# First and last mixture layers: experts rounded to 64 rows, 36 blocks with 4 shared ones; middle layer's shared-block weights copied on chip

## The chip, the cores and the metric

The kernel runs on one core of one Trainium2 chip. The metric is the device time of one execution in microseconds, lower is better. The chip's engines that matter here are TensorE (PE in the profile, its weight loads are PEld), VectorE (DVE), ScalarE (ACT), GpSimd (POOL) and SyncE (SP, which only issues transfers).

## The reference

Four layers over x of 4 x 512 tokens of 256 numbers; each adds an attention and then a feed-forward part. Three of the feed-forward parts are mixtures of experts in which every token goes to 2 experts:

```
x = x + attention(layernorm(x), ctx)                     # each layer has its own kind
# layers 0 and 3: 8 experts, hidden size F = 704 and 512
scores -> two experts per token, weights w0, w1
y = sum over the token's experts of w * (silu(t @ gate[e]) * (t @ up[e])) @ down[e]
x = x + y
# layer 1: 7 routed experts of F = 256 (the same form) and one shared expert that all tokens pass
# layer 2: one fp4-quantised feed-forward part, no experts
```

2048 tokens x 2 experts are 4096 (token, expert) pairs. All arithmetic of the experts is float32.

## The kernel before, in words

The stages run one behind another: `a0` (attention), `e0` (experts, F = 704), `a1`, `l1` (attentions), `e1` (experts, F = 256), `f2`, `a3`, `e3` (experts, F = 512). Between stages, and between the parts of a stage, all engines meet at a barrier.

**Routing** (`route`, tags e0r, e1r, e3r). VectorE works out for each pair a slot in a list of blocks of 128 rows, and for each block the expert that owns it (`owner`) and the token in each row (`token`). A matmul with one-hot matrices makes `token`. In e0 and e3 every expert's rows are rounded up to 128, which takes at most `ROUTED` = 39 blocks, each with one owner. The simple arithmetic for that stands at L2148 to L2163. In e1 a `Layout` of quarters (32 rows) is used: 34 blocks, of which 28 are whole and 6 are *mixed*: four experts with 32 rows each. Its arithmetic is longer (L2165 to L2197).

**Blocks of e0 and e3** (`blocks`, tags e0b, e3b). The down weights of all experts are kept in SBUF. Gate and up weights of one block's expert (F = 704: two transfers of 704 KB; F = 512: two of 512 KB) go into one of two buffers, `e0k_wgu` and `e0b_wgu` (e3k_wgu, e3b_wgu). SP waits until the up product of block n is done (`up_made`) and then reads the owner of block n+2 and issues its load (L1870 to L1872) into the buffer that block n has just left. PE does for block n: gate product (L2386, weights stationary and tokens moving, 128 columns at a time), transpose of the rows of block n+1 (L2380, `xp`), up product (L2386), down product of block n-1 (L2410, `yp`). ACT does silu of the gate (L2446), VectorE copies the turned rows (L2458), multiplies up by silu into `hT` (L2465), and weighs the result into `yb` (L2473). With F = 704 (`LEFT` is 64) the gate product of block n+1 waits for `h_done` of block n, since its bank also holds the last 64 columns of the up product. POOL fetches the rows of a block by an indirect transfer (L2345), its pairs' weights (L2351), and adds `yb` into `y_sum` by an indirect transfer that adds (L2359); each such send waits until the one before has landed. All four loops are hardware loops, the order of the blocks is 0, 1, 2, ... In e0, VectorE also does one `round` of fp4 quantisation for a later stage after every second block (18 in all).

**Blocks of e1** (`kept_blocks`, tag e1b). All experts' weights stay in SBUF (`e_kgu`, `kept_d`). Rows are stationary and weights move: a whole block takes two matmuls over 512 columns for gate and up (L2584), a mixed block eight, with 32 stationary columns each (L2581), and likewise for down (L2607, L2604). The four experts' weights of a mixed block are loaded again from HBM by SP into `e1b_mixed_gu`, `xn` and others (L2532), two sets at the beginning and then one behind each mixed block. POOL copies the row numbers to `e1b_index`, runs a filler instruction and fetches the rows (L2547 to L2550), from the first block on; ACT issues the stores of the results (L2639). PE runs 14 filler matmuls (`stay_busy`) first. The order of PE is gate and up of n, turn of the rows of n+1 (L2568), turn of the hidden rows of n-1 (L2594), down of n-2.

## Time and profile before

| | us |
|---|---|
| median of 3 runs | 1716.93 (1716.62 to 1720.66) |
| the profiled execution, whole | 1715.14 |
| its span, first to last instruction | 1713.2 |
| PE busy | 1485.6 (87%) |
| DVE, ACT, POOL busy | 945.3, 498.5, 485.1 |
| blocks of e0, first gate product to end of the last down product | 179.0 to 484.4 |
| blocks of e1, same | 974.1 to 1089.3 |
| blocks of e3, same | 1477.4 to 1695.2 |

The three stretches of blocks are 638 us of the span. The rest of the chip's time, 1.9 us of the profiled execution, lies outside the span. A timeline merges instructions of one line that follow one another: start, length, engine, line, what is written and read, how many, and in brackets the idle time of the engine before them with what ended it. One float32 product shows as two MATMUL records.

### The profile page before, as it was taken

What the parts mean: (1) busy time and instruction counts of PE and PEld (TensorE: products, weight loads), DVE (VectorE), ACT (ScalarE), POOL (GpSimd) and SP (SyncE); (2) the same over time, 40 slices, a digit from 0 to 9 for tenths busy, and PEclk for the clock granted to TensorE, in tenths of its full rate; (3) what the DMA queues carried; (4) which work ended last, traced back from release to release, by engine and by line L of the source; (5) the groups of instructions that cost most, each with busy time, mean ns of one, the idle gap of its engine ahead of it and who ended that gap; (6) DMA issues with size and microseconds to landing.
All of it is one profiled execution on the core that took longest, in us unless ns stands there. A gap on an engine that the chain in (4) does not pass through costs nothing. (4 is left out here: it accounts for less than half of the span.)

```text
span 1713.2 us, 33545 instructions
## 1 busy us (share of the span) xinstructions
PE 1485.6 (87%) x11942; PEld 1126.6 (66%) x11975; DVE 945.3 (55%) x2428; ACT 498.5 (29%) x1047; POOL 485.1 (28%) x585
## 2 busy tenths in 40 slices
PE   4887899999979986899978899677888797899995
PEld 3664799999968853455545455345666575699995
DVE  4556244444448968666637433489887556422221
ACT  2331111111147745465532122223331333011010
POOL 0102344444410002111112243342111110466663
PEclk9999999999988997899999999888899999999998
DMA  4209677777720005433305467210000004688885
GB/s 139 51 2 308 218 210 232 210 230 213 222 59 1 2 2 165 130 89 112 86 22 197 143 212 260 67 45 25 1 1 1 2 2 156 197 242 234 233 241 147
DMA packets 147445, 218.73 MB, mean 128 GB/s; under 512 B 21377, under 2 KB 96897, under 8 KB 147137
## 3 DMA queue, kind: packets, MB, share of 16 engines
q1 hardware_dynamic: 121792, 183.57, 32.9%
q0 software_dynamic: 20640, 29.16, 8.2%
q10 hardware_dynamic: 4896, 4.46, 0.8%
q8 instruction: 72, 1.18, 0.3%
q14 instruction: 45, 0.36, 0.1%
HBM read 184.59 MB, written 34.64 MB: 128 GB/s over the span
## 5 line engine op out<-in xcount | busy, mean ns | idle before, releaser
L1575 DVE TENSOR_REDUCE l1a_nm<-l1a_sc 128x1 f32<-128x512 f32 (+3 forms) x256 | 107.2, 483 | 53.6 <-PE l1a_sc L1711 53.6
L2446 ACT ACTIVATE e0b_sg<-e0b_gp 128x640 f32<-128x640 f32 x78 | 33.5, 481 | 266.1 <-PE e0b_gp L2386 266.1
L2359 POOL DMA_INDIRECT y_sum<-e0b_yb,e_token x39 | 63.1, 1619 | 140.5 <-DVE e0b_yb L2473 137.5
L2359 POOL DMA_INDIRECT y_sum<-e3b_yb,e_token x39 | 62.7, 1607 | 61.5 <-DVE e3b_yb L2473 58.6
L2446 ACT ACTIVATE e3b_sg<-e3b_gp 128x512 f32<-128x512 f32 x39 | 23.3, 597 | 189.5 <-PE e3b_gp L2386 189.5
L1709 PEld LDWEIGHTS l1a_sc<-l_stack_k,l_stack_q 128*128 128x128 bf16 x256 | 25.3, 99 | 60.9 <-issue 26.9
L1711 PE MATMUL l1a_sc<-causal_h,ident_h 128*128 128x128 bf16 x256 | 47.0, 223 | 19.9 <-PEq L1353 15.5
L2465 DVE TENSOR_TENSOR e0b_hT<-e0b_up,e0b_sg 128x640 f32<-128x640 f32 x39 | 32.2, 825 | 57.8 <-PE e0b_up L2386 57.8
L2753 POOL TENSOR_TENSOR f_hq<-f_q,f_q 128x704 f32<-128x704 f32 x16 | 22.9, 1432 | 135.7 <-DVE f_q L2740 135.7
L1470 POOL TENSOR_TENSOR xn<-xn 128x512 f32<-128x512 f32 x8 | 10.1, 1266 | 178.2 <-DVE xn L1438 178.2
L2386 PEld LDWEIGHTS e0b_gp<-e0b_xT,e0k_wgu 128*128 128x128 f32 x480 | 58.4, 197 | 1.9 <-DVE e0b_xT L2458 0.9
L1245 DVE TENSOR_REDUCE a_nm<-a_sc 128x8 f32<-128x512 f32 x64 | 39.7, 683 | 35.8 <-PE a_sc L1095 35.8
L2386 PE MATMUL e0b_gp<-e0b_xT,e0k_wgu 128*128 128x128 f32 x480 | 58.7, 281 | 0.5 <-DVE e0b_xT L2458 0.5
L2465 DVE TENSOR_TENSOR e3b_hT<-e3b_up,e3b_sg 128x512 f32<-128x512 f32 x39 | 27.0, 692 | 57.6 <-PE e3b_up L2386 57.6
L2584 PE MATMUL e1b_gu<-e_kgu,e1b_xT 128*128 x112 | 54.8, 613 | 1.8 <-DVE e1b_xT L2661 1.8
L1737 PE MATMUL l1a_st<-l_stack_q,l_stack_k 128*128 128x512 bf16 (+2 forms) x254 | 56.1, 302 | 0.0
L2386 PEld LDWEIGHTS e0b_gp<-e0b_xT,e0b_wgu 128*128 128x128 f32 x456 | 53.8, 192 | 2.5 <-issue 1.5
L2386 PE MATMUL e0b_gp<-e0b_xT,e0b_wgu 128*128 128x128 f32 x456 | 54.1, 276 | 1.4 <-DVE e0b_hT L2465 1.4
L2473 DVE TENSOR_SCALAR e0b_yb<-e0b_yp,e0k_weight 128x256 f32<-128x256 f32 x39 | 18.9, 484 | 62.4 <-PE e0b_yp L2410 62.4
L3236 PE MATMUL f_yp<-f2w_down,f_hT 128*128 128x256 f32 x192 | 49.1, 410 | 4.6 <-DVE x L3091 4.0
L1189 POOL CAST a_nmp<-a_nm 128x32 bf16<-128x32 f32 x16 | 8.9, 553 | 153.7 <-DVE a_nm L1245 153.7
L1709 PE MATMUL l1a_sc<-l_stack_k,l_stack_q 128*128 128x256 bf16 (+3 forms) x226 | 50.4, 297 | 1.8 <-DVE l1a_nm L1575 1.5
(637 smaller groups left out, 4015.1 us busy)
## 6 DMA issues: line engine op xcount, KB each, us to landing
e3k_wgu<-in_L_ffn_W SPq DMA_DIRECT2D x40, 512.0 KB
e3b_wgu<-in_L_ffn_W SPq DMA_DIRECT2D x38, 512.0 KB
e0k_wgu<-in_L_ffn_gate_proj SPq DMA_DIRECT2D x20, 704.0 KB
e0k_wgu<-in_L_ffn_up_proj SPq DMA_DIRECT2D x20, 704.0 KB
e0b_wgu<-in_L_ffn_gate_proj SPq DMA_DIRECT2D x19, 704.0 KB, 4.2
e0b_wgu<-in_L_ffn_up_proj SPq DMA_DIRECT2D x19, 704.0 KB, 5.5
x_rows<-xn SPq DMA_DIRECT2D x3, 2048.0 KB, 8.4
l_parts<-l1p_split SPq DMA_DIRECT2D x16, 384.0 KB, 3.1
```

What stands on the lines that cost most here:

```text
L1245: nc.vector.tensor_reduce(nm[:, :, r, :], bank[r][:].rearrange("p t (h l) -> p t h l", l=L), AX_X, ALU.max, negate=True).then_inc(max_done, 1)
L1575: nc.vector.tensor_reduce(nm[:, g % 2, q, i:i + 1], sc[q], AX_X, ALU.max, negate=True).then_inc(max_done, 1)
L1709: nc.tensor.matmul(sc[q], of_head(1, n)[:, q * P:(q + 1) * P], of_head(0, n)[:, 0:(q + 1) * P], start=True, stop=False)
L1711: last = nc.tensor.matmul(sc[q][:, q * P:(q + 1) * P], ident_h[:], causal_h[:], start=False, stop=True)
L1737: nc.tensor.matmul(to(k), of_head(0, n)[:, k * P:(k + 1) * P], of_head(1, n)[:, k * P:], start=False, stop=False)
L2359: pool.indirect_dma_start(y_sum, bass.IndirectOffsetOnAxis(ap=token[:, n:n + 1], axis=0), yb[n % 2][:], None, compute_op=ALU.add).then_inc ...
L2386: last = nc.tensor.matmul(dst[:, f, :], wgu[j][:, k, at + f * P:at + (f + 1) * P], xT[j][:, k, :], start=(k == 0), stop=(k == KC - 1))
L2446: last = nc.scalar.activation(sg[rows, chunks, :], gp[rows, chunks, :], ACT.Silu)
L2465: last = nc.vector.tensor_tensor(hT[j][rows, chunks, :], from_up, sg[rows, chunks, :], ALU.mult)
L2584: last = nc.tensor.matmul(gu[n % 2][:], xT[n % 2][:, k, :], wgu[:, bass.ds(e, 1), k, :].rearrange("p a f -> p (a f)"), start=(k == 0), sto ...
L2753: nc.gpsimd.tensor_tensor(v3(dst), v3(a[:, 0:n]), bcast(sc[:, 0:n // FP4_BLOCK], 2, FP4_BLOCK), ALU.mult).then_inc(result, 1)
L3236: last = nc.tensor.matmul(yp[:], hT[:, f, :], dT[:, f, :], start=(f == 0), stop=(f == FC - 1))
```

## The change

**Layout.** e0 and e3 get a `Layout` of halves: experts are rounded to 64 rows, 36 blocks, of which 32 are whole and 4 are mixed: rows 0 to 63 of one expert, rows 64 to 127 of another. The mixed blocks stand at places 4, 13, 22 and 31. Routing of e0 and e3 takes the longer arithmetic that e1 had, with 40 owners, and three more VectorE instructions for `plan.send`, the rows' targets per owner: in a mixed block each half is sent by an instruction of its own, the other half's rows going to a spare area.

**Blocks of e0 and e3.** All loops are written out. A *unit* is one owner's gate and up weights; there are 40 units for 36 blocks. Unit k goes to buffer k % 2 and its load waits for the up product of the block that used unit k-2. A mixed block n uses both buffers. Its gate and up products have the tokens stationary, 64 columns for each expert, and the weights moving, up to 512 columns; the hidden rows then have to be turned (`turn_hidden`, into a new bank `hp`), ACT copies them to `hT`, and the down product of block n follows at once, not one block later. Down weights of its two experts are copied in SBUF by ACT, piece by piece between the silus of the blocks before.

**Blocks of e1.** The layout stays (34 blocks, 6 mixed). The mixed blocks' weights are copied from the kept ones by ACT instead of being loaded; the stores are issued by SP; POOL's index copy and filler are gone; the rows of blocks 0 and 1 are fetched already in routing; the 14 filler matmuls are gone.

```diff
+HALVES = Layout(NE, P // 2)
+ROUTED = HALVES.blocks
...
+                        for n in range(2):
+                            pool.indirect_dma_start(first_rows[n][:], None, x_rows, bass.IndirectOffsetOnAxis(ap=token[:, n:n + 1], axis=0))\
...
-                    with sp.Fori(0, (NB - 3) // 2) as i:
-                        for j in (1, 0):
-                            step(i * 2 + 2 - j, j)
+                    for k in range(1, len(block_of)):
+                        if k >= 2:
+                            sp.wait_ge(up_made, block_of[k - 2] + 1)
+                        plan.load_gate_up(sp, owner, owner_of[k], k % 2)
...
+                        for i, (block_n, at, done, value) in enumerate(sent):
+                            if block_n == n:
+                                if i:
+                                    pool.wait_ge(*sent[i - 1][2:])
+                                pool.indirect_dma_start(y_sum, bass.IndirectOffsetOnAxis(ap=plan.send[:, at:at + 1], axis=0), yb[n % 2][:],
+                                                        None, compute_op=ALU.add).then_inc(done, 16)
...
+                                for k in range(KC):
+                                    for u, unit in enumerate(units_of[n]):
+                                        rows = slice(u * HALF, (u + 1) * HALF)
+                                        last = nc.tensor.matmul(flat(dst)[rows, lo:hi], xT[n % 2][:, k, rows],
+                                                                wgu[unit % 2][:, k, at + lo:at + hi], start=(k == 0), stop=(k == KC - 1))
...
+                        for unit in units_of[n]:
+                            pe.wait_ge(gu_in[unit % 2], 32 * (unit // 2 + 1))
...
+                        elif not is_mixed(n - 1):
+                            down(n - 1)
+                        if is_mixed(n):
+                            turn_hidden(n)
+                            down(n)
...
+                        for to, source in itertools.islice(pieces, 2 * FC // 3):
+                            nc.scalar.copy(to, source).then_inc(mixed_ready, 1)
...
-                        nc.gpsimd.tensor_copy(index[n % 2][:], token[:, order[n]:order[n] + 1]).then_inc(index_ready, 1)
-                        pool.wait_ge(index_ready, n + 1)
-                        nc.gpsimd.tensor_tensor(spare[:], const("place"), const("place"), ALU.add)
...
-                    stay_busy(gu[0][:], 14)
...
-                        if n >= 3:
-                            store(n - 3)
+                        if n in mixed_at and following:
+                            pieces = set_of(following[0])
+                        if following:
+                            copy_some(pieces, -(-OF_SET // (mixed_at[following[0]] - 1 - (mixed_at[following[0] - 1] if following[0] else 0))))
```

PE in e3, before: one block of the written-out first pass of the loop, which all blocks repeat. `gp` and `up` are the banks of the gate and up products, `inner` and `xnT` hold the kept down weights.

```order
L2386 MATMUL e3b_gp<-e3b_xT,e3b_wgu 128x128 x8
L2403 TENSOR_LOAD e_owner
L2403 ISA x2
L2380 MATMUL e3b_xp<-consts,e3k_xb 128x128 x2
L2386 MATMUL e3b_up<-e3b_xT,e3b_wgu 128x128 x8
L2410 ISA
L2410 MATMUL e3b_yp<-inner,e3b_hT 128x256
```

PE in e3 of the change, at the first mixed block: from the end of the down product of block 2 to the gate product of block 5.

```order
L2447 MATMUL e3b_yp<-xnT,e3b_hT 128x256
L2403 MATMUL e3b_gp<-e3k_wgu,e3b_xT 64x512
L2403 MATMUL e3b_gp<-e3b_wgu,e3b_xT 64x512
...
L2393 MATMUL e3b_xp<-consts,e3k_xb 128x128 x2
L2403 MATMUL e3b_up<-e3k_wgu,e3b_xT 64x512
...
L2447 MATMUL e3b_yp<-xnT,e3b_hT 128x256
L2429 MATMUL e3b_hp<-consts,first_weights 128x128 x4
L2441 MATMUL e3b_yp<-first_weights,e3b_hT 64x256 x8
L2408 MATMUL e3b_gp<-e3b_xT,e3k_wgu 128x128 x8
```

The mixed block reads both weight buffers from its first gate matmuls on, the turn and the down product of its own follow the down product of block 3, and nothing but the turn of block 6's rows stands between the gate and up products of block 5 and the gate product of block 6.

ACT in e1, before, at the first blocks: silu (L2646), copy of the turned hidden rows (L2635), store.

```order
L2646 ACTIVATE e1b_sg<-e1b_gu 128x256 x2
L2635 COPY e1b_hT<-e1b_hp 128x256
L2646 ACTIVATE e1b_sg<-e1b_gu 128x256
L2635 COPY e1b_hT<-e1b_hp 128x256
L2639 DMA y_slots<-e1b_yb 128x256
```

ACT in e1 of the change, the same place; behind the first silu come six copies of 512 columns, behind the second six of 256.

```order
L2685 TENSOR_LOAD e_owner
L2685 ISA x2
...
L2697 COPY e1b_mixed_gu<-e_kgu 128x512
L2707 ACTIVATE e1b_sg<-e1b_gu 128x256
L2697 ISA
L2697 COPY e1b_mixed_gu<-e_kgu 128x512
...
L2707 ACTIVATE e1b_sg<-e1b_gu 128x256
L2680 COPY e1b_hT<-e1b_hp 128x256
L2697 ISA
L2697 COPY e1b_mixed_d<-inner 128x256
```

The silus and copies of the hidden rows now stand behind up to six weight copies, and no store is left on ACT.

## Rows read from the trace of the kernel before

**Rows 1.** Timeline of PE, e0: start, length, what, idle before.

```profile
178.99 4.67 PE L2386 MATMUL e0b_gp<-e0b_xT,e0k_wgu 128*128 128x128 f32 x24 [0.52 <-DVE e0b_xT L2458]
...
187.50 2.92 PE L2386 MATMUL e0b_gp<-e0b_xT,e0b_wgu 128*128 128x128 f32 x24 [1.39 <-DVE e0b_hT L2465]
...
195.30 2.84 PE L2386 MATMUL e0b_gp<-e0b_xT,e0k_wgu 128*128 128x128 f32 x24
...
200.42 1.03 PE L2410 MATMUL e0b_yp<-inner,e0b_hT 128*128 x4
...
203.02 2.84 PE L2386 MATMUL e0b_gp<-e0b_xT,e0b_wgu 128*128 128x128 f32 x24
```

**Rows 2.** Timeline of PE, e3, down product to gate product one block on.

```profile
1491.93 1.03 PE L2410 MATMUL e3b_yp<-inner,e3b_hT 128*128 x4
...
1493.66 1.95 PE L2386 MATMUL e3b_gp<-e3b_xT,e3b_wgu 128*128 128x128 f32 x16
1495.45 0.38 PE L2380 MATMUL e3b_xp<-consts,e3k_xb 128*128 128x128 f32 x2
1495.67 1.95 PE L2386 MATMUL e3b_up<-e3b_xT,e3b_wgu 128*128 128x128 f32 x16
1497.45 1.03 PE L2410 MATMUL e3b_yp<-inner,e3b_hT 128*128 x4
```

**Rows 3.** Timeline of SP, e3: the next issue of weights.

```profile
1492.95 0.89 SPq L1872 DMA_DIRECT2D e3k_wgu<-in_L_ffn_W  x2
```

**Rows 4.** Chain that ended last, e3's beginning: start, length, what.

```profile
1476.36 0.38 SPq L1872
...
1476.85 4.83 DMA e3b_wgu<-in_L_ffn_W
```

**Rows 5.** Transfers by issuer: count, KB each, median us to landing.

```profile
e0b_wgu<-in_L_ffn_up_proj SPq DMA_DIRECT2D x19, 704.0 KB, 5.5
...
y_sum<-e3b_yb,e_token POOLq DMA_INDIRECT x39, 4.4
e1b_xb<-x_rows,e1b_index POOLq DMA_INDIRECT x34, 4.3
```

**Rows 6.** Timeline of PE, e1.

```profile
974.05 3.34 PE L2584 MATMUL e1b_gu<-e_kgu,e1b_xT 128*128 x4 [0.81 <-DVE e1b_xT L2661]
...
988.50 1.92 PE L2581 MATMUL e1b_gu<-e1b_mixed_gu,e1b_xT 128*32 128x512 f32 x16
...
991.72 1.88 PE L2584 MATMUL e1b_gu<-e_kgu,e1b_xT 128*128 x4
...
994.74 1.88 PE L2584 MATMUL e1b_gu<-e_kgu,e1b_xT 128*128 x4
...
1084.06 1.92 PE L2581 MATMUL e1b_gu<-xn,e1b_xT 128*32 128x512 f32 x16
```

**Rows 7.** Timeline of e1's beginning: fillers, first rows fetched and turned.

```profile
966.02 3.19 PE L359 MATMUL e1b_gu<-ones_h,ident_h 128*128 128x512 bf16 x14 [1.74 <-PEq L2003]
...
972.81 0.44 PE L2568 MATMUL e1b_xp<-consts,e1b_xb 128*128 128x128 f32 x2 [3.59 <-DMA e1b_xb<-x_rows,e1b_index]
```

**Rows 8.** Timeline of DVE: counts to owners, e0's routing, then e1's.

```profile
152.83 0.17 DVE L2148 COPY e0r_cnt<-e0r_small 128x8 f32<-128x8 f32 x1 [1.11 <-PE e0r_small L2020]
...
156.24 0.17 DVE L2221 CAST e_owner<-e0r_own 128x39 int32<-128x39 f32 x1
...
935.80 0.16 DVE L2165 TENSOR_SCALAR e1r_held_i<-e1r_small 128x8 uint32<-128x8 f32 x1
...
941.45 0.21 DVE L2225 TENSOR_TENSOR e_owner<-e1r_own,e1r_wrap 128x52 int32<-128x52 f32 x1
```

**Rows 9.** Groups of ACT: count, busy us, mean ns, idle before.

```profile
L2446 ACT ACTIVATE e0b_sg<-e0b_gp 128x640 f32<-128x640 f32 x39 | 27.4, 703 | 266.1 <-PE e0b_gp L2386 266.1
L2635 ACT COPY e1b_hT<-e1b_hp 128x256 f32<-128x256 f32 x34 | 12.7, 372 | 9.0 <-PE e1b_hp L2594 7.8
...
L1413 ACT CAST l1p_split<-xn 128x512 bf16<-128x512 f32 x16 | 9.4, 613 | 0.7 <-DVE xn L1447 0.5
```

More of the change, by code:

```diff
@@ L8 @@
+import itertools
 from contextlib import ExitStack
@@ L2397, in up_product @@
-                    def up_product(n, j):
-                        if positive(n):
+                        product(0, FC, gp, n, gate_made)
+                    def up_product(n):
+                        if n:
                             pe.wait_ge(h_done, n)
-                        product(F + LEFT, FULL, up, j, up_made)
-                    def expert(n):
-                        return pe.value_load(owner[0:1, bass.ds(n, 1)], min_val=0, max_val=plan.E - 1)
-                    def down(n, j, e):
-                        if positive(n):
-                            pe.wait_ge(y_copied, n)
-                        pe.wait_ge(h_done, n + 1)
-                        for f in range(FC):
-                            last = nc.tensor.matmul(yp[:], hT[j][:, f, :],
-                                                    plan.wd[f // 2][:, bass.ds(e, 1), f % 2, :].rearrange("p a d -> p (a d)"),
-                                                    start=(f == 0), stop=(f == FC - 1))
-                        last.then_inc(y_made, 1)
@@ L2415, in body @@
-                    def body(i, last_block=False):
-                        for j in (1, 0):
-                            n = i * 2 + 2 - j
-                            gate(n, j, i + 2 - j)
-                            e = expert(n - 1)
-                            if not (last_block and j == 0):
-                                turn_rows(n + 1, 1 - j, i + 2)
-                            up_product(n, j)
-                            down(n - 1, 1 - j, e)
-                    stay_busy(gp[:, 0:4, :].rearrange("p f c -> p (f c)"), 4)
@@ L2426, in _ @@
[L2426 to L2437 removed]
+                        product(F + LEFT, FULL, up, n, up_made)
@@ L2439, in _, with weights_of @@
+                    if not is_mixed(NB - 1):
+                        down(NB - 1)
                 @block.scalar
                 def _(act):
+                    def weights_of(i):
+                        for u, at in enumerate(lay.owner_at(order[mixed_at[i]])):
+                            e = act.value_load(owner[0:1, at:at + 1], min_val=0, max_val=plan.E - 1)
+                            for f in range(FC):
+                                yield mixed_d[u][:, f * D:(f + 1) * D], \
+                                    plan.wd[f // 2][:, bass.ds(e, 1), f % 2, :].rearrange("p a d -> p (a d)")
@@ L2445, in silu, with copy_hidden @@
+                        last.then_inc(sg_done, 1)
+                    def copy_hidden(n):
+                        act.wait_ge(h_turned, mixed_at.index(n) + 1)
                         for rows, chunks in PIECES:
-                            last = nc.scalar.activation(sg[rows, chunks, :], gp[rows, chunks, :], ACT.Silu)
-                        last.then_inc(sg_done, 1)
+                            last = nc.scalar.copy(hT[n % 2][rows, chunks, :], hp[rows, chunks, :])
+                        last.then_inc(h_done, 1)
@@ L2489, in _ @@
-                    body(0)
-                    with dve.Fori(1, NB // 2 - 1) as i:
-                        body(i)
-                    body(NB // 2 - 1, last_block=True)
-                    weigh_out(NB - 1, 0, NB // 2)
-    def kept_blocks(tag, wgu, wd, kept, F, lay, experts_n, owner, token, weights):
+                    copy_rows(0)
+                    for n in range(NB):
+                        if n + 1 < NB:
+                            copy_rows(n + 1)
+                        hidden(n)
+                        if n >= 1 and not is_mixed(n - 1):
+                            weigh_out(n - 1)
+                        if is_mixed(n):
+                            weigh_out(n)
+                        if rounds is not None and n % 2:
+                            rounds.round(dve, n // 2)
@@ L2510, in kept_blocks @@
             xp, hp = ps("xp", [P, 2 * KC, P]), ps("hp", [P, 2 * FC, P])
[L2511 to L2512 removed]
+            before = list(blocks_before)
+            blocks_before[0] += (NB + 1) // 2
+            blocks_before[1] += NB // 2
             mixed_gu = [tmp("mixed_gu", [P, PER, KC, 2 * F]),
```

465 lines of the change are left out of this document (251 added, 214 removed).

## The prediction

> **What bounds the kernel now.** I read three views, in this order: the timeline of PE through the blocks of e0 and e3, the issue of weights by SP beside it, and the same for e1. In e0 a block is 7.72 us of PE from one gate product to the next (195.30 to 203.02) with no idle time inside; its down product is the last 2.60 us of it (200.42 to 203.02) [rows 1]. In e3 a block is 5.52 us: down 1.73 (1491.93 to 1493.66), gate, turn and up 3.79 (to 1497.45), of these gate 1.79, turn 0.22, up 1.78, and then the next down [rows 2]. So there PE is the bound, block after block, and a block saved is worth its PE time, as long as everything that PE needs is there. What it needs from HBM is the block's weights. They are issued 1.02 us after the up product before (1491.93 to 1492.95) [rows 2, 3], and land 5.3 us after the first issue (1476.36 to 1476.85 + 4.83 = 1481.68) [rows 4]. In e0 the second of the two transfers takes 5.5 us from its own issue [rows 5], which comes some 0.5 us after the first, as SP needs 0.89 us for two [rows 3]: 6.0 us. Today this is hidden, because the load for block n+2 starts at the end of the up product of block n and has a down product and a whole block to run: 1.73 + 5.52 = 7.25 us in e3 against 1.02 + 5.3 and a wake-up of some 0.25, 6.6 us. The cover is only 0.7 us long. That margin is the centre of this prediction.
>
> e1 is not at its PE limit: a whole block is 3.02 us when nothing is missing (991.72 to 994.74), 3.22 when mixed (988.50 to 991.72), but from the first gate product to that of the last block, 33 blocks, it takes 110.0 us (974.05 to 1084.06) [rows 6], 3.33 each; rows land only 4.3 us after issue there [rows 5], and behind an index copy and a filler on POOL. It also begins late: PE's fillers start at 966.02, the first rows are there at 972.81 after 3.59 us of idle time [rows 7], and the first gate product runs at 974.05 and takes 3.34 us instead of 1.88 [rows 6].
>
> **Blocks saved.** 39 become 36: 3 x 7.72 = 23.2 us in e0 and 3 x 5.52 = 16.6 us in e3 come off [rows 1, 2]. A mixed block streams as many columns in total per half as a whole one if its two halves run side by side. No row shows two tiles of 64 columns; the nearest has four of 32 side by side, 16 records of 512 columns in 1.92 us beside 4 records in 1.88 [rows 6]. So I count a mixed block as a whole one plus 0.2 us (3.22 less 3.02) for each of its three products, 0.6.
>
> The Trainium skill (TensorEngine Tiling (Array Packing), Key Properties) says that a change of the tiling mode drains the engine, which speaks against four mixed blocks between whole ones; the trace puts all of that at the 0.2 us above, so by its rule the sum stays as it is.
>
> **What each mixed block costs, first wait.** A mixed block needs both weight buffers. The second is in use by block n-1 until its up product ends, and only then SP issues the load. PE has nothing left but the down product of block n-2. In e3: 1.0 + 5.3 + 0.25 - 1.73 = 4.9 us of idle time (rounded up from 4.8); in e0: 1.0 + 6.0 + 0.2 - 2.6 = 4.6 us. SP's written-out loop might issue 0.3 earlier; a queue that still moves rows might land 0.7 later: 4.3 to 5.6 each.
>
> **Second wait: its own hidden rows.** After the down product of n-1 PE turns the hidden rows, 0.11 us per transpose (0.22 for two [rows 2]): 6 in e0, 0.7; 4 in e3, 0.4. Then it waits for ACT's copy. ACT takes 703 ns for 640 columns [rows 9] and another small piece in e0, some 0.59 for 512 between that and the 372 ns of 256; with hand-overs both ways I take 1.3 in e0 and 1.0 in e3. The multiplication by VectorE ahead of it is hidden by the down product of n-1.
>
> **Third wait: the block behind.** Both next units wait for the same up product of the mixed block. In e3 the first is there 6.6 us after it; PE has down 1.73, turns 0.4, wait 1.0, down 1.73, 4.9 in all, so it waits 1.7 again. It then runs gate to up (3.8, to 10.4) and goes on at once, for there is no down product left; the second unit, whose transfer follows the first, is there. The up product at 10.4 releases the next load, which lands at 17.0; PE is through at 10.4 + 3.8 + 1.73 = 15.9: 1.1 more. In e0 the first load is covered (6.0 + 1.2 against 2.6 + 0.7 + 1.3 + 2.6), but the gate product of n+2 waits for VectorE's hidden rows of n+1 with no down product over it; that is what the second block of the stage shows today, 1.39 us [rows 1], 1.4.
>
> Sum per mixed block: e0 4.6 + 0.7 + 1.3 + 1.4 + 0.6 = 8.6; e3 4.9 + 0.4 + 1.0 + 1.7 + 1.1 + 0.6 = 9.7. Times four: 34.4 and 38.8. Against the blocks saved: e0 **+11.2**, e3 **+22.2**.
>
> **The clock.** The waits of 4.6 and 4.9 us are long enough to matter once more. After 3.59 us of idle time [rows 7] e1's first gate product took 3.34 instead of 1.88 us [rows 6], and e0's first, which also came behind a stop, took 4.67 instead of 2.84 [rows 1]: the lower of the two clock levels, 1.2 GHz, for some microseconds. The losses are 1.46 and 1.83, 1.6 in the mean. With eight such waits, one for each mixed block of e0 and e3: **+12.8**, from 0 (the level never falls) to 27 (twice as long each time).
>
> The Trainium skill (TensorE: Matmul & The Clock Gate, Part 1) calls the low level the default, which activity lifts and waits for transfers bring back; the two rows agree, and a sum without it is the second rival.
>
> **Other work.** Routing: e0's chain from the counts to the owners is 156.24 - 152.83 = 3.4 us, the longer one in e1 is 941.45 - 935.80 = 5.65 [rows 8]; less a little for 600 instead of 676 comparisons, 2.1 us more, in e0 and in e3: **+4.2** (3 to 6, with the three instructions for the targets). The 18th quantisation round now comes after the last pair of blocks, before the last weighing; no row prices what the last down product leaves uncovered, 0 to 3 us, I take **+0.9**. The second send of a mixed block costs POOL up to 4.4 us of landing [rows 5] and an issue; fetches stand behind it, but are wanted only some two blocks later, and PE's own waits give that time: 0.
>
> **e1.** Rows of block 0 are there before PE comes; from its start at 966.0 one turn and copy (972.81 to 974.05 today, 1.24) lead to a gate product at 967.3. From there to the gate product of the last block, 33 x 3.02 = 99.7, 1.0 for five mixed blocks on the way; the missing down products of the first two and the bubbles in their place cancel: end at 1068. ACT has to carry 16 copies per set: 613 ns for 512 columns [rows 9] and some 0.4 for 256, 8 x 0.61 + 8 x 0.4 = 8.1 us. At four in a block that is 2.5 + 0.38 + 0.37 = 3.3 us in the blocks with wide copies against 3.02 of PE, and reading four owners comes on top behind each mixed block; the slack of the hidden rows, some 2 us, takes most of it. I count 2 us, range 0 to 8. 1084.06 - 1070 = 14: **-14.3** with 0.3 for the smaller one-hot tables in routing; range -8 to -18. The removed fillers cost nothing, since PE comes from the shared expert's products without a long stop.
>
> **Sum.** 11.2 + 22.2 + 12.8 + 4.2 + 0.9 - 14.3 = 37.0. On the profiled execution's 1715.1 that is 1752. The median of the runs, 1716.9, is 1.8 higher: **1754**.
>
> **Rivals.**
> - *Clock stays up.* The same waits, no fall in the clock, or in few of them: 24 us more than before, 1741. For it: the wait is between dense products. Against: the 3.59 us one.
> - *The waits are not there, the kernel becomes faster.* One mechanism: the load of a mixed block's second unit lands within the down product. Without the first and third waits (4 x 4.6 + 4 x 7.7 = 49 us) and their clock (13), the sum is 37 - 62 = -25: 1692. It decides from a point: faster than before needs the first wait with its clock below some 1.6 us per mixed block with all the rest as worked out, so a load that is issued a down product earlier. The wait on `up_made` as written speaks against it.
> - *The two halves run one after another.* Then gate, up and down of a mixed block double: 7.5 us in e0, 5.3 in e3, 51 us in all: 1805. The four tiles of e1 speak against it.
> - *ACT bounds e1.* Six wide copies before the second silu and owner reads: the gain shrinks to 6: 1762.
>
> **How the numbers follow.** Forecast, 1745 to 1770 with ACT's rival inside: 0.62. Clock stays up, 1726 to 1745: 0.20. Waits mostly covered, anything down to 1692: 0.13, of which 0.08 is faster by more than 0.3% (5 us, about what a measurement of this kernel can tell from no change) and 0.05 within it. Halves in turn: 0.04, other 0.01. The range of 8 in 10 goes from 1724 to 1770. Slower by over 0.3%: 0.87.
>
> **What would show it.** Right: four idle times of PE of 4 to 5 us in e0 and in e3 before records of the mixed gate product, put down to a weight transfer, and slow records behind them; about 1.3 and 1.0 before the mixed down product; 1.4 in e0 before the gate product two blocks on; blocks of e1 at 3.0 to 3.1 us, starting at once. Wrong: a mixed gate product without idle time before it; mixed products at twice the length of whole ones; e1's PE waiting for ACT.

## The result and the profile after

The changed kernel takes **1772.1 us** (median of 4 runs, 1766.1 to 1779.1) against 1716.8 of the kernel before (4 runs, 1713.7 to 1720.7): a ratio of 1.0307, 95% interval 1.0272 to 1.0342, 55 us slower. The forecast was 1754, slower, with a range to 1770: the sign and the mechanism hold, the size is 18 us short, and the measured median lies 2 us above the top of the range.

The profiled execution spans 1770.2 us against 1713.2. By stages, from the starts and ends of TensorE's products in the two timelines (the first gate product of a stage to the end of its last down product):

| stretch | before | after | difference | forecast |
|---|---|---|---|---|
| start to e0's first gate | 179.0 | 181.9 | +2.9 | +2.1 |
| e0's blocks | 305.5 | 325.2 | +19.7 | +18.5 |
| e0's end to the next stage | 6.4 | 9.8 | +3.5 | 0 |
| to the shared expert's end in e1 | 473.4 | 474.9 | +1.5 | 0 |
| shared expert to e1's first gate | 9.8 | 2.9 | -6.9 | -14.3 |
| e1's blocks | 115.2 | 110.7 | -4.5 | (with the row above) |
| e1's end to e3's first gate | 388.1 | 394.1 | +6.0 | +2.1 |
| e3's blocks | 217.8 | 251.3 | +33.5 | +28.6 |
| e3's end to the end | 17.9 | 19.3 | +1.4 | 0 |

Two rows need a word. e0's difference hides 1.7 us: its first gate product ran at the low clock level before (4.67 us) and at the high one after (2.94). That isn't the change's doing: e1_alone (below), whose e0 is the old one, has the high level there too (6.8 us to the next gate product, against 8.5 before). Of the +6.0 between e1 and e3, e3's routing takes 2.9 and the stop behind e1 1.4. But e1_alone, whose routing in e3 is the old one, has 394.2 us there too, because its stage f2 takes 240.8 us against 235.6; in the thirteen traces f2 takes anything between these two. A stage of a single profile is good to a few us.

Three stretches of the kernel after, e0, e1 and e3: start and end, length, busy time and instructions of PE, PEld, DVE, ACT and POOL, granted clock, DMA share, GB/s.

```profile
181.90:507.00 325.10, 294.19 (x2110) 259.18 (x2110) 126.60 (x322) 48.64 (x124) 132.06 (x109) 0.97 0.67 204
994.76:1105.50 110.74, 109.75 (x550) 61.11 (x550) 39.39 (x100) 63.62 (x164) 30.22 (x32) 0.97 0.25 77
1499.57:1750.90 251.33, 216.17 (x1494) 182.35 (x1494) 56.70 (x106) 34.30 (x72) 129.20 (x108) 0.96 0.70 201
```

In e0 PE is idle 31 of 325 us, in e3 35 of 251; before it was 2 us in each. The clock is 0.97 and 0.96 in them, 0.99 and 1.00 before. In e1 the opposite: PE has 1 us of idle time, and the DMA share is 0.25, since the mixed weights no longer come from HBM.

**The first mixed block of e0**, which answers to [rows 1]: the timeline of PE.

```profile
211.06 1.03 PE L2447 MATMUL e0b_yp<-xnT,e0b_hT 128*128 x4
216.38 0.61 PE L2403 MATMUL e0b_gp<-e0k_wgu,e0b_xT 128*64 128x512 f32 x1 [4.29 <-DMA e0b_wgu<-in_L_ffn_up_proj]
216.38 0.64 PE L2403 MATMUL e0b_gp<-e0b_wgu,e0b_xT 128*64 128x512 f32 x1
216.83 0.59 PE L2403 MATMUL e0b_gp<-e0k_wgu,e0b_xT 128*64 128x512 f32 x1
...
218.02 1.06 PE L2403 MATMUL e0b_gp<-e0k_wgu,e0b_xT 128*64 128x512 f32 x1
218.09 1.06 PE L2403 MATMUL e0b_gp<-e0b_wgu,e0b_xT 128*64 128x512 f32 x1
218.88 0.63 PE L2403 MATMUL e0b_gp<-e0k_wgu,e0b_xT 128*64 128x256 f32 x1
...
226.16 0.82 PE L2429 MATMUL e0b_hp<-consts,first_weights 128*128 128x128 f32 x6
228.01 0.40 PE L2441 MATMUL e0b_yp<-first_weights,e0b_hT 128*64 128x256 f32 x1 [1.03 <-ACT e0b_hT L2495]
...
230.75 2.94 PE L2408 MATMUL e0b_gp<-e0b_xT,e0k_wgu 128*128 128x128 f32 x24
233.53 0.38 PE L2393 MATMUL e0b_xp<-consts,e0k_xb 128*128 128x128 f32 x2
233.75 2.40 PE L2408 MATMUL e0b_up<-e0b_xT,e0k_wgu 128*128 128x128 f32 x20
237.53 2.92 PE L2408 MATMUL e0b_gp<-e0b_xT,e0b_wgu 128*128 128x128 f32 x24 [1.39 <-DVE e0b_hT L2530]
```

Read it from the top. The down product of block 2 ends at 212.1; PE waits 4.29 us for the second unit's weights. The products of the two halves start together, 0.45 us from pair to pair at first (216.38 to 216.83): two tiles of 64 columns do run side by side. Then the pairs come 0.86 apart (218.02 to 218.88), the level of 1.2 GHz, and the granted clock is at that level for 20.5 us in all within e0 and as long within e3, against 3.7 and 0 before. The turn takes 0.82, the wait for ACT's copy 1.03, the gate product of the next block comes without a wait, and the one after that waits 1.39 for VectorE.

Who waited for whom, PE in e0 and then in e3 (us in total, times, longest):

```profile
PE e0b_gp L2403 <- DMA e0b_wgu<-in_L_ffn_up_proj: 18.6, 4, 5.5
PE e0b_gp L2408 <- DVE e0b_hT L2530: 6.9, 5, 1.4
PE e0b_yp L2441 <- ACT e0b_hT L2495: 4.1, 4, 1.0
PE e0b_yp L2447 <- DVE e0b_yb L2538: 1.3, 1, 1.3
```

```profile
PE e3b_gp L2403 <- DMA e3b_wgu<-in_L_ffn_W: 19.4, 4, 5.3
PE e3b_gp L2408 <- issue: 8.0, 10, 1.5
PE e3b_yp L2441 <- ACT e3b_hT L2495: 3.1, 4, 0.8
PE e3b_xp L2393 <- DMA e3k_xb<-x_rows,e_token: 2.8, 2, 1.8
```

The first wait is 4.65 us each in e0 and 4.85 in e3; 4.6 and 4.9 were forecast. Waits "<- issue" in e3 are waits for weights too: behind the first mixed block those ahead of the gate products at 1539.28 (1.30 us) and 1549.43 (0.61 us) end 0.09 us after the weights have landed. From gate product to gate product a mixed block and its two neighbours take 12.2 + 14.4 + 6.8 us in e0, where three whole ones take 23.2, and 10.4 + 13.0 + 3.9 + 6.3 in e3, where four take 22.1.

**e1's beginning**, which answers to [rows 7] and the first lines of [rows 6]: the timeline of PE.

```profile
984.78 7.07 PE L1931 MATMUL e1s_yp<-e1s_wd,xn 128*128 128x256 f32 x32
993.62 0.43 PE L2613 MATMUL e1b_xp<-consts,e_xb 128*128 128x128 f32 x2 [1.77 <-PEq L2005]
994.76 3.00 PE L2628 MATMUL e1b_gu<-e_kgu,e1b_xT 128*128 x4 [0.71 <-DVE e1b_xT L2723]
...
998.79 3.76 PE L2628 MATMUL e1b_gu<-e_kgu,e1b_xT 128*128 x4 [0.60 <-DVE e1b_xT L2723]
```

The rows are there when PE comes. But two gate products run slowly (3.00 and 3.76 us against 1.9 later): the level is low here too. The same stops don't always bring that: in fewer_blocks (below), behind stops of 1.74 and 0.71 us, the first gate product takes 1.98 us. From the third block on a whole block takes 3.02 us.

### The profile page after: what moved, and what is told of

It reads as the page before. It is cut to its first block and busy times, and to the rows that moved or that the text cites. A ratio compares the mean times of both kernels' runs of the same rounds, so it can differ in the third digit from the quotient of the medians.

```text
span 1770.2 us, 31734 instructions
## 1 busy us (share of the span) xinstructions
PE 1480.7 (84%) x11668; PEld 1071.8 (61%) x11668; DVE 938.3 (53%) x2435; ACT 562.8 (32%) x1222; POOL 460.5 (26%) x507
## 5 line engine op out<-in xcount | busy, mean ns | idle before, releaser
L2372 POOL DMA_INDIRECT y_sum<-e0b_yb,e0k_send x40 | 64.6, 1616 | 133.1 <-DVE e0b_yb L2538 91.8
L2489 ACT ACTIVATE e0b_sg<-e0b_gp 128x640 f32<-128x640 f32 x64 | 27.5, 481 | 192.6 <-PE e0b_gp L2408 192.6
L2372 POOL DMA_INDIRECT y_sum<-e3b_yb,e3k_send x40 | 64.6, 1615 | 86.9 <-DMA y_sum<-e3b_yb,e3k_send 54.2
L1715 PE MATMUL l1a_sc<-l_stack_k,l_stack_q 128*128 128x512 bf16 (+3 forms) x256 | 59.1, 309 | 17.4 <-PEq L1359 15.7
L2517 DVE COPY e3b_xT<-e3b_xp 128x256 f32<-128x256 f32 x36 | 15.3, 425 | 98.7 <-PE e3b_xp L2393 98.7
L1743 PE MATMUL l1a_st<-l_stack_q,l_stack_k 128*128 128x512 bf16 (+3 forms) x256 | 56.6, 302 | 0.0
L2517 DVE COPY e0b_xT<-e0b_xp 128x256 f32<-128x256 f32 x36 | 15.2, 422 | 74.4 <-PE e0b_xp L2393 74.4
L2408 PE MATMUL e0b_gp<-e0b_xT,e0b_wgu 128*128 128x128 f32 x384 | 45.8, 276 | 6.9 <-DVE e0b_hT L2530 6.9
L2594 POOL DMA_INDIRECT e_xb<-x_rows,e_token x32 | 30.2, 944 | 79.5 <-PE e1b_xp L2613 68.9
L2408 PEld LDWEIGHTS e0b_gp<-e0b_xT,e0b_wgu 128*128 128x128 f32 x384 | 45.0, 192 | 8.3 <-issue 7.7
L2530 DVE TENSOR_TENSOR e3b_hT<-e3b_up,e3b_sg 128x512 f32<-128x512 f32 x32 | 22.1, 692 | 47.6 <-PE e3b_up L2408 47.6
```

The source lines that it names most:

```text
L1715: nc.tensor.matmul(sc[q], of_head(1, n)[:, q * P:(q + 1) * P], of_head(0, n)[:, 0:(q + 1) * P], start=True, stop=False)
L1743: nc.tensor.matmul(to(k), of_head(0, n)[:, k * P:(k + 1) * P], of_head(1, n)[:, k * P:], start=False, stop=False)
L2372: pool.indirect_dma_start(y_sum, bass.IndirectOffsetOnAxis(ap=plan.send[:, at:at + 1], axis=0), yb[n % 2][:], None, compute_op=ALU.add).th ...
L2408: last = nc.tensor.matmul(dst[:, f, :], wgu[units_of[n][0] % 2][:, k, at + f * P:at + (f + 1) * P], xT[n % 2][:, k, :], start=(k == 0), st ...
L2489: last = nc.scalar.activation(sg[rows, chunks, :], gp[rows, chunks, :], ACT.Silu)
L2517: nc.vector.tensor_copy(xT[n % 2][:], xp[:]).then_inc(x_copied, 1)
```

## The experiments

All times are medians, the difference is that to the kernel before on the same chip (whose medians were 1717.3 to 1720.2). The changed kernel stands at +55.3.

**e1_alone.** The kernel before with e1's part alone: `kept_blocks` as changed, and in `route`

```diff
+                    if first_rows is not None:
+                        pool.wait_ge(first_routed, 1)
+                        pool.wait_ge(sent, 16)
+                        for n in range(2):
+                            pool.indirect_dma_start(first_rows[n][:], None, x_rows, ...).then_inc(rows_in[n], 16)
```

> The kernel before, with e1's part of the change alone (first two row fetches issued in the routing stage, mixed weights copied by ScalarE, rows turned ahead). If the e1 term of the forecast holds, 14.3 us under before: about 1702.5. By the two traces, the gap between the last shared product and gate(0) went from 9.77 to 2.91 us and the blocks from 115.25 to 110.74 us: 11.4 us under before, about 1705. If the gain in e1 is given back at the stage borders behind it: 1712 or more.

Measured: 1708.3 us, -10.9; ratio 0.9938 (0.9919 to 0.9958). In its trace the gap ahead of the first gate product is 2.9 us and e1's blocks take 109.3. The e1 part stands alone, is a gain, and is nearer to the 11.4 of the traces than to the forecast's 14.3. This kernel is faster than the one before and the changed one.

**busy_wait.** The changed kernel; TensorE fills the wait ahead of each mixed gate product.

```diff
+                        if is_mixed(n):
+                            stay_busy(flat(gp)[:, 0:S], 16)
                         for unit in units_of[n]:
                             pe.wait_ge(gu_in[unit % 2], 32 * (unit // 2 + 1))
```

> The changed kernel with 16 small matmuls on TensorE (3.4 us) into the gate bank ahead of each mixed gate, while it waits for weights anyway. The granted clock should stay at 1.0 through the mixed blocks. If low clock costs half of the low stretches seen in e0 and e3 (20.6 and 20.5 us, part of them idle): 8 to 13 us under the changed kernel, 1759 to 1764. If the time is set by the loads and by what is behind the mixed block and the slow products are hidden: within 3 us of 1772.

The wait for the gate bank, into which the fillers write, now stands ahead of that for the weights, in every block.

Measured: 1755.5 us, +36.3; ratio 1.0235 (1.0189 to 1.0282). That is 17 to 19 us under the changed kernel by the medians, and 12, good to some 10, by the ratios; the stages below are the better measure. The timeline of PE at the same mixed gate product as above:

```profile
213.94 3.62 PE L365 MATMUL e0b_gp<-ones_h,ident_h 128*128 128x512 bf16 x16
218.48 0.61 PE L2403 MATMUL e0b_gp<-e0k_wgu,e0b_xT 128*64 128x512 f32 x1 [0.93 <-DMA e0b_wgu<-in_L_ffn_up_proj]
...
220.22 0.38 PE L2403 MATMUL e0b_gp<-e0k_wgu,e0b_xT 128*64 128x256 f32 x1
...
220.44 0.38 PE L2403 MATMUL e0b_gp<-e0k_wgu,e0b_xT 128*64 128x256 f32 x1
```

The wait is as long (3.62 + 0.93), the product behind it is not slow: 256 columns come 0.22 us apart, not 0.42. The granted clock is 1.00 in both stages, e0's blocks take 317.8 us (7.4 less) and e3's 244.1 (7.2 less). So the clock's share in the blocks is 14.6 us, or some 16, since e0's first gate product had the low level here and the high one in the changed kernel (8.4 and 6.8 us to the next). It was on the critical path; the forecast had 12.8. The Trainium skill (TensorE: Matmul & The Clock Gate, Part 1) says that waits for transfers bring the low level back; these two kernels agree, and show what it costs here.

**three_buffers.** The changed kernel with the second unit's weights loaded one block earlier.

```diff
-                        if k >= 2:
-                            sp.wait_ge(up_made, block_of[k - 2] + 1)
-                        plan.load_gate_up(sp, owner, owner_of[k], k % 2)
+                        if k >= 3:
+                            sp.wait_ge(up_made, block_of[k - 3] + 1)
+                        plan.load_gate_up(sp, owner, owner_of[k], k % 3)
```

> The changed kernel with a third buffer for gate and up weights, so that both units of a mixed block are loaded while the block ahead runs (in e0 the copy of the second unit's down weights goes to the tile x, which is idle there, to make room). If the load wait ahead of the mixed gate and the low clock behind it are the cost: 4 x (4.3 + 1.6) in e0 and 4 x (5.3 + 1.3 + 1.6) in e3 come back, about 1716 to 1722. If in e3 the chain of sends on GpSimd is late next, only e0's part: about 1747. If the 64-row products themselves cost it: 1772.

Measured: 1730.7 us, +11.4; ratio 1.0076 (1.0052 to 1.0101). It lies between the first expectation and the second. It gives back 44 us of the 56 that the load theory had for it; no PE wait over 0.2 us for gate or up weights is left behind the first blocks. What a mixed block costs beyond whole ones falls to 4.1 us in e0 (12.7 + 6.8 against 15.4; the last one 6.8) and 2.0 in e3 (9.2 + 3.9 against 11.1). e3's blocks take 226.7 us, and there the chain on GpSimd, without effect so far, comes up: three steps of 10.8, 11.6 and 9.3 us between gate products, each with a late row fetch. The timelines of POOL and PE at the first:

```profile
1522.26 1.63 POOL L2374 DMA_INDIRECT y_sum<-e3b_yb,e3k_send  x1 [0.43 <-issue]
...
1524.19 0.98 POOL L2364 DMA_INDIRECT e3k_weight<-w_pairs,e3k_pair  x1 [0.30 <-issue]
...
1525.48 0.95 POOL L2356 DMA_INDIRECT e3k_xb<-x_rows,e_token  x1 [0.30 <-issue]
...
1526.61 0.44 PE L2395 MATMUL e3b_xp<-consts,e3k_xb 128*128 128x128 f32 x2 [3.36 <-DMA e3k_xb<-x_rows,e_token]
```

POOL issues without a pause (send 1.6, weight 1.0, rows 1.0 us, 0.3 between them, and waits for sends to land), and PE waits 3.36 us for rows. GpSimd has become the late one.

**one_send.** The changed kernel without the second send of each mixed block.

```diff
-                for at in lay.owner_at(order[n]):
+                for at in lay.owner_at(order[n])[:1]:
                     summed[n % 2] += 1
```

> The changed kernel without the second send of each mixed block: the rows of its second half are left out of the sum. If the second send with its wait on the first (6.4 us between their starts) holds up GpSimd's row and weight fetches in e3, as waits of 1.0 to 2.0 us for rows and up to 3.0 us for row weights behind mixed blocks suggest: 8 to 14 us under the changed kernel, 1758 to 1764. If TensorE's own waits hide it, as the forecast had it: within 3 us of 1772.

Measured: 1769.2 us, +49.9; ratio 1.0302 (1.0257 to 1.0347), which can't be told from the changed kernel's 1.0307 (1.0272 to 1.0342). e3's blocks take 250.7 us against 251.3. The rows that made the send suspect are these, POOL in e3 of the changed kernel, first and second send of a mixed block and the fetches behind them:

```profile
1543.73 1.63 POOL L2372 DMA_INDIRECT y_sum<-e3b_yb,e3k_send  x1 [0.99 <-DMA y_sum<-e3b_yb,e3k_send]
1550.18 1.58 POOL L2372 DMA_INDIRECT y_sum<-e3b_yb,e3k_send  x1 [4.83 <-DMA y_sum<-e3b_yb,e3k_send]
1552.07 1.01 POOL L2362 DMA_INDIRECT e3k_weight<-w_pairs,e3k_pair  x1 [0.30 <-issue]
1553.39 0.99 POOL L2354 DMA_INDIRECT e3k_xb<-x_rows,e_token  x1 [0.30 <-issue]
```

The second send keeps POOL for 6.4 us, and still costs next to nothing. PE waits for weights at the same place; the forecast's 0 holds for the changed kernel, and no longer once the weights are early.

**piped.** The changed kernel, two buffers, but `turn_hidden` of a mixed block behind the gate product of the next block and its `down` behind the up product of the next.

```diff
+                        if n and is_mixed(n - 1):
+                            turn_hidden(n - 1)
                         up_product(n)
...
-                        elif not is_mixed(n - 1):
-                            down(n - 1)
-                        if is_mixed(n):
-                            turn_hidden(n)
-                            down(n)
+                        else:
+                            down(n - 1)
```

> The changed kernel with a mixed block's turn of the hidden rows behind the gate product of the next block and its down product behind the up product of the next, in place of right behind its own up product; two weight buffers as in the changed kernel. If the waits inside a mixed block (turn 0.8, wait for the copied hidden rows 1.0, wait for the hidden rows ahead of the next gates 1.4) are costs of their own: 4 x 3 in e0 and 4 x 2 in e3 come back, about 1752. If the loads set the pace, the wait for the next block's weights grows by what the reordering takes out: 1766 to 1772.

Measured: 1800.0 us, +82.6; ratio 1.0460 (1.0415 to 1.0505). Neither expectation: 27 us slower than the changed kernel. Its waits of PE in e0 and its timeline show why:

```profile
PE e0b_gp L2403 <- DMA e0b_wgu<-in_L_ffn_up_proj: 18.5, 4, 5.5
PE e0b_gp L2408 <- issue: 15.9, 4, 4.1
```

```profile
229.53 4.54 PE L2408 MATMUL e0b_gp<-e0b_xT,e0k_wgu 128*128 128x128 f32 x24 [4.04 <-issue]
...
234.13 0.82 PE L2433 MATMUL e0b_hp<-consts,first_weights 128*128 128x128 f32 x6
```

The turn, its wait and the down product of the mixed block (4.6 us, 226.16 to 230.75 in the changed kernel) stood where the next block's weights were being loaded. Moved away, they uncover a second wait of 4.0 us, which ends 0.09 us after the weights have landed (229.44), behind which that gate product runs at the low clock level again (4.54 instead of 2.94 us), and are still to be done. What looked like a cost of the mixed block was cover.

**piped3.** Both edits: third buffer and later turn.

> Both edits together: a third weight buffer and the mixed block's turn and down product behind the next block's products. From three_buffers (1730.7): what is left there of a mixed block beyond two whole ones is 4.1 us in e0 and 2.0 us in e3; if most of it goes, about 1712. If GpSimd's chain of sends and row fetches sets e3's pace (three bubbles of 3.8 to 6.1 us in three_buffers, each with a late row fetch behind a send), e3 gains nothing: 1718 to 1722.

Measured: 1722.0 us, +4.7; ratio 1.0036 (1.0004 to 1.0068). A mixed block now costs 1.3 us beyond a whole one in e0 (8.1 + 8.6 against 15.4) and 1.0 in e3 (5.9 + 6.2 against 11.1), turn included. The Trainium skill (TensorEngine Tiling (Array Packing), Key Properties) has a change of tiling mode drain the engine; if it does, it is inside this 1.0. e0's blocks take 291.7 us, 13.8 less than before, but e3's 228.1, 10.3 more: eight late row fetches, 11.3 us in all. So the second expectation holds, e3 gains nothing. Of e0's 13.8 us, 1.7 are again the first gate product's clock level.

**piped3_deep.** piped3 with three row and three output buffers; on GpSimd

```diff
-                        fetch(n)
-                        if n >= 4:
-                            send(n - 4)
-                            fetch_weight(n - 2)
+                        if n + 1 < NB:
+                            fetch(n + 1)
+                        if n >= 3:
+                            fetch_weight(n - 1)
+                        if n >= 5 and is_mixed(n - 5):
+                            send(n - 5, 1)
+                        if n >= 4:
+                            send(n - 4, 0)
```

> piped3 with three row buffers and three output buffers in e0 and e3, each block's rows and row weights fetched one block earlier, ahead of the send, and the second send of a mixed block one block later than the first. If the order on GpSimd is what is late in e3 once the weights are early, its bubbles (15 us in three_buffers) go: 1695 to 1700, under e1_alone's 1708. If the sends themselves, one waiting for the other, can't keep up with a block in 5.5 us: as piped3.

Measured: 1730.7 us, +13.4; ratio 1.0064 (1.0035 to 1.0094); e3's blocks 230.4. PE's waits in e3:

```profile
PE e3b_yp L2474 <- DVE e3b_yb L2565: 12.2, 4, 5.2
PE e3b_xp L2416 <- DMA e3k_xb<-x_rows,e_token: 3.9, 3, 1.8
```

Rows are late less, 5.2 us with those into the third buffer; in their place PE waits 12.2 us for the weighing, and that for an output buffer whose send has not landed. The kernel is also 9 us slower than piped3, where the second expectation had the same time: the stage behind e0 starts 16.9 us after e0's last product, against 11.4, since the last sends come later. So fetching earlier gains nothing: the chain of sends, each waiting for the one before, holds the output buffers. That no other order on GpSimd could do better isn't shown.

**whole_blocks.** The changed kernel, its e0 and e3 rounded to 128 rows.

```diff
+WHOLES = Layout(NE, P)
...
-        lay = QUARTERS if shared else HALVES
+        lay = QUARTERS if shared else WHOLES if tag in ('e0', 'e3') else HALVES
```

> The changed kernel with e0 and e3 rounded to 128 rows again (39 whole blocks, none mixed); its routing steps, its written-out blocks in place of the loops, and its e1 stay. If the rounding to 64 rows is what costs: the kernel before, less 11.4 for e1, plus 4.2 for the routing steps, about 1710. GpSimd's drain at the end of e0 and e3 took 4.4 and 4.6 us before and 8.5 us in every kernel with the changed blocks; if that comes from the written-out code it is 8.5 us here too and the time about 1714; if it comes from the mixed blocks' sends it is back at 4.4.

Measured: 1717.4 us, -1.9; ratio 0.9985 (0.9968 to 1.0001). Against e1_alone that is 9.0 us for the routing steps and the written-out code. e3's blocks take 226.2 us against 219.7 in e1_alone. PE's waits ahead of e3's gate products, here and in e1_alone:

```profile
PE e3b_gp L2412 <- issue: 4.3, 6, 1.2
```

```profile
PE e3b_gp L2395 <- issue: 0.5, 1, 0.5
```

GpSimd's drain (the instruction that ends its part of a stage; its time spans the last send) is back at 4.6 us; in the changed kernel it takes 8.5. Where it shows is the start of the stage behind e0, timelines of PE of the kernel before, the changed one, this one and fewer_blocks (below):

```profile
490.83 3.75 PE L708 MATMUL a_sc<-ctxT,fm_signs 128*128 128x256 f32 x8 [6.37 <-PEq L2318]
```

```profile
516.92 3.75 PE L714 MATMUL a_sc<-ctxT,fm_signs 128*128 128x256 f32 x8 [9.85 <-PEq L2332]
```

```profile
493.66 3.75 PE L716 MATMUL a_sc<-ctxT,fm_signs 128*128 128x256 f32 x8 [5.95 <-PEq L2336]
```

```profile
475.63 3.75 PE L716 MATMUL a_sc<-ctxT,fm_signs 128*128 128x256 f32 x8 [9.68 <-PEq L2336]
```

**fewer_blocks.** whole_blocks without the last three blocks of e0 and e3.

```diff
-        NB, HALF = lay.blocks, lay.unit
+        NB, HALF = lay.blocks - 3, lay.unit
...
-        order = lay.order(centred=True)
+        order = lay.order(centred=True)[:NB]
```

> whole_blocks with the last three blocks of e0 and of e3 left out, so 36 whole ones each; the rows of those blocks are not summed. If a block is worth its TensorE time where no mixed one comes in: 3 x 7.72 + 3 x 5.52 = 39.8 us under whole_blocks, about 1677.5. If loads or sends set part of the pace in e3, less: 1682 or more. GpSimd's drain at the end of e0 is 4.6 us in whole_blocks and 8.5 with mixed blocks; 8.5 here would put it to the number of blocks, 4.6 to the mixed ones.

Measured: 1682.6 us, -37.7; ratio 0.9792 (0.9769 to 0.9816); 35.8 less than whole_blocks, at the edge of the second expectation, but not for its reason. e0's blocks take 23.2 us less, as forecast to the tenth, e3's 21.0 less, more than 16.6 (whole_blocks' own waits above are in that: against e1_alone's 219.7 it is 14.5 less). But GpSimd's drain is 8.3 us and PE starts the next stage 3.7 us later. So the long drain goes with the 36 blocks, not with the mixed ones: in one_send, with one send for each of the 36, it is 8.4 too. Part of a drain is the last send, which lands 3.9 to 4.1 us after the drain's start in either case. Behind 39 blocks (115 indirect transfers by GpSimd) the drain ends 0.5 us after that landing, in all nine such stages of the traces. Behind 36 blocks it ends 4.4 us after it with 106 transfers (one_send, fewer_blocks) and 4.5 us after it with 110, in all seventeen.

**pe_written_out.** e1_alone with one line changed.

```diff
-                    with pe.Fori(1, NB // 2 - 1) as i:
+                    for i in range(1, NB // 2 - 1):
                         body(i)
```

> e1_alone with one line changed: TensorE's loop over the pairs of blocks in e0 and e3 is written out block by block, as the changed kernel has it; all other engines as in e1_alone. e3's 39 whole blocks took 219.7 us in e1_alone and 226.2 in whole_blocks, where six steps between gate products are 6.1 to 6.9 us long instead of 5.5 and 14 instruction transfers of 16 KB fall into the stage instead of 3. If TensorE's longer code is the reason: e3's blocks at about 226 us, about 14 such transfers, and some 1715 against e1_alone's 1708. If not: e3's blocks at 218 to 220 us and 1708.

Measured: 1709.8 us, -10.4; ratio 0.9950 (0.9932 to 0.9968), as e1_alone. The DMA queue of instructions within e3's blocks (queue, packets, MB, share), in e1_alone, here and in whole_blocks:

```profile
q8 instruction: 3, 0.05, 0.1%
```

```profile
q8 instruction: 14, 0.23, 0.4%
```

```profile
q8 instruction: 14, 0.23, 0.4%
```

The transfers of 16 KB are TensorE's longer code, that part was right. But e3's blocks take 221.8 us, 2.1 more, with two steps of 6.3 and 6.4 us, and the median doesn't move: TensorE's code explains 2 of the 6.5 us at most. The trace says what the two steps wait for: their gate products start 0.09 us after their weights have landed, 7.0 us after the issue. It is the margin of 0.7 us that the prediction worked out for e3's loads; why a load is late now and then isn't shown.

**halves_e0.** e0 in the form of piped3, e3 with whole blocks, e1 as changed.

> e0 with 32 whole and 4 mixed blocks in the form of piped3 (third weight buffer, turn and down product of a mixed block behind the next block's products), e3 with 39 whole blocks, e1 as changed. In piped3 e0's blocks took 291.7 us against 305.5 before. If that gain stands alone, whole_blocks less 13.8: about 1698 to 1702, under e1_alone. If the stage borders and routing give it back: as e1_alone, about 1708, or more.

Measured: 1716.9 us, -2.3; ratio 0.9985 (0.9970 to 0.9999). e0's blocks take 298.8 us: the mixed blocks are as cheap as in piped3 (8.1 + 8.6), but two other steps take 11.9 and 13.7 us instead of 7.7, each with a row fetch 2.6 and 2.9 us late. The stage behind starts 3.8 us later than in whole_blocks. Of the 5.6 us that e0 gains on whole_blocks in these profiles the border takes 3.8. So the second case holds, on its "or more" side, and e1_alone stays the fastest complete kernel.

## Why the forecast was right, and where it fell short

The experiments give the forecast's sum term by term, each from two kernels' differences to the kernel before. By the intervals the rows are good to 5, 7, 4 and 3 us. They add up to the whole by the way they are formed, so the sum proves nothing; what each row says is the finding. The late quantisation round stands in the first row, since only kernels of 36 blocks have it.

| term | forecast | measured | from |
|---|---|---|---|
| blocks saved, with the late round | -38.9 | -35.8 | fewer_blocks less whole_blocks |
| eight mixed blocks in place of whole ones, clock included | +86.0 | +93.0 | changed less fewer_blocks |
| routing, written-out code | +4.2 | +9.0 | whole_blocks less e1_alone |
| e1 | -14.3 | -10.9 | e1_alone |
| sum | +37.0 | +55.3 | |

- **Blocks saved.** Right in e0 (23.2 us). The miss is at the border: GpSimd's drain at the end of e0 takes 8.5 us with 36 blocks, 4.4 with 39, and the next stage waits for it, 3.5 to 3.8 us: PE starts 0.28 us after the drain's end, before (490.55) and after (516.64). The prediction gave e0's end 0.9 us for a quantisation round; the last down product did wait 1.3 us for the weighing before it, but the drain wasn't in it at all. At the end of the kernel the tail grew by 1.4 us, the drain there runs beside the writing of the result.
- **First wait, second wait, third wait in e0.** Right, and in size: 4.65 and 4.85 us for the first (4.6 and 4.9), 0.82 + 1.03 against 0.7 + 1.3 for turn and copy in e0, 0.60 + 0.8 against 0.4 + 1.0 in e3, 1.39 for the hidden rows (1.4). The 0.25 us taken from a load's landing to the product stands in no row; the traces show 0.09. three_buffers shows that the waits for weights (the first one, and e3's third) with their clock are the main cost: 44 us of the mixed blocks' 93.
- **Third wait in e3.** Right in kind, oversized: 7.4 of the 8.0 us "<- issue" stand behind mixed blocks, 1.8 us for each, where 1.7 + 1.1 were forecast. In its place come late rows, 2.8 us in all, which had no term. Against fewer_blocks, which has 36 written-out blocks too and none mixed, a mixed block costs 11.0 us in e0 ((325.2 - 281.2) / 4) and 11.5 in e3 ((251.3 - 205.2) / 4), its clock included. The forecast had 8.6 + 1.6 = 10.2 and 9.7 + 1.6 = 11.3.
- **Clock.** Right. +12.8 forecast, 14.6 by busy_wait's two stages (16 with e0's start taken alike), 12 to 19 by its runs. The rival "clock stays up" is out.
- **Halves side by side.** Right, pairs start together, and a mixed block costs 1.0 to 1.3 us in all once the waits are gone (piped3), of which the turn is 0.6 and 0.8; 0.6 was forecast for its products.
- **Second send: 0.** Right for this kernel (one_send), for the reason given. It is the next bound behind the weights (three_buffers, piped3, piped3_deep).
- **Routing and written-out code.** The chain from the counts to the owners grew as worked out: from 156.11 to 161.69 in e0's routing, 5.6 us against 3.4 in [rows 8]. But no term was there for the blocks being written out instead of looped: e3's 39 whole blocks take 226.2 instead of 219.7 us. The waits say where: 4.3 us ahead of gate products against 0.5. In pe_written_out (2.1 us of the 6.5) and fewer_blocks the long ones end 0.09 us after the weights have landed, so loads there came later than their 0.7 us of cover allowed; for whole_blocks that is inferred. Why the loads are late stays open, as the other engines' code wasn't tried one by one, and a single profile of a stage can be off by a few us.
- **e1.** The start is right to 0.1 us (gap 9.8 to 2.9; forecast 6.75 earlier). The blocks gained 4.5 us here instead of 7.3, 5.9 in e1_alone: the price of the low clock at the start, two slow gate products, was left out, because the fillers' removal was costed at nothing "since PE comes without a long stop". It stopped for 1.77 and 0.71 us, and they were slow, 3.0 us together. In fewer_blocks the level stayed high behind the same stops, so this price is partly luck.
- **Faster if waits are covered.** That rival named the point: a load issued a down product earlier. three_buffers does more than that and still ends 11 us slower: e3's sends take over, and the terms outside the mixed blocks were 11 us too small. The rival was wrong in taking the sum of waits as the gain; 62 us were to come back, 44 did, and with the turn hidden as well 51.

What stays open: why the drain goes on for 4 us behind the last landing with 36 blocks and not with 39, and why loads are late now and then in e3 once the blocks are written out.

## What to carry to other kernels

Fewer, fuller blocks save the engine's time but not the loads and the sends: 36 blocks with 4 shared ones need 40 weight loads and 40 sends where 39 blocks needed 39, so where a stage has under 1 us of cover on its loads (0.7 us here), count buffers per block first, and price the clock with the wait. Before moving work out of a place that looks like a cost, look at which transfer it covers; piped made that mistake for 27 us. Try the independent parts of a change alone: here the middle stage's part, 11 us, made the fastest kernel, and the rest hid it.

## What the runs showed of the hardware

- Waits of 4.2 to 5.5 us within an otherwise full stage brought TensorE to the 1.2 GHz level at every one of the eight mixed blocks, and 3.6 us of fillers in the wait kept it at 2.4 GHz: 14.6 us for eight waits. Stops of 1.7 and 0.7 us at e1's start went with the low level in most traces (first gate product 3.35 us in e1_alone) and not in fewer_blocks (1.98).
- Products of 64 columns and 512 moving numbers on the two halves of the array start together, 0.45 us from pair to pair (216.38 to 216.83), and cost about as much as one of 128 columns: four records of e1's whole gate products take 1.88 us, 0.43 from start to start.
- GpSimd's drain at the end of a stage took 4.4 to 4.6 us behind 39 blocks and 8.3 to 8.7 behind 36, in e0 and e3 of all thirteen traces, whether mixed or not; behind e0 TensorE starts the next stage 0.28 us after it (before and after). The last send lands 3.9 to 4.1 us after its start, and what follows that landing is 0.5 us with 115 indirect transfers, 4.4 with 106 and 4.5 with 110. The cause isn't known.
- TensorE's code for 39 written-out blocks came in as 14 transfers of 16 KB in one stage instead of 3, with 2.1 us more in the blocks and no difference in the median that the runs could tell (-10.4 and -10.9 us to the kernel before).
